# Experts by halves of the batch, with the second attention's beginning between the later phases

## The reference

```python
capacity = max(1, int(Sz * CAP_FACTOR / E) + 1)
scores = jax.nn.softmax(jnp.einsum('bsd,ed->bse', x, router_w), axis=-1)
gate_vals, sel_idx = jax.lax.top_k(jnp.swapaxes(scores, 1, 2), capacity)
tokens = x[b_idx, sel_idx]
h = jax.nn.gelu(jnp.einsum('becd,edh->bech', tokens, w1) + b1[None, :, None, :], approximate=False)
y = jnp.einsum('bech,ehd->becd', h, w2) + b2[None, :, None, :]
out = jnp.zeros_like(x).at[b_idx, sel_idx].add(y * gate_vals[..., None])
```

## Time and profile before

| | |
|---|---|
| median of three runs | 796.57 us |
| span of the profiled execution | 801.9 us (its only time; no other is given for it) |
| PE busy | 644.6 us, 80% of the span |
| DVE busy | 548.5 us, 68% |
| POOL busy | 361.2 us, 45% |
| ACT busy | 353.9 us, 44% |
| mean granted clock of PE | 0.925 of full speed |

### The profile page before, as it was taken

One profiled execution on the slowest core, in us unless ns is written; L12 is line 12 of the kernel. 1 busy time (PEld: TensorE's weight loads), 2 busy tenths in 40 slices (PEclk: granted clock), 3 DMA queues, 4 the chain that ended last, 5 costly groups with the idle time before them and its releaser, 6 DMA issues.

```text
span 801.9 us, 14622 instructions
## 1 busy us (share of the span) xinstructions
PE 644.6 (80%) x4312; PEld 398.9 (50%) x4345; DVE 548.5 (68%) x1808; ACT 353.9 (44%) x764; POOL 361.2 (45%) x513
## 2 busy tenths in 40 slices
PE   1489898997206699999795569899999999999795
PEld 1246666664103478877584223454545454544453
DVE  8378888888691133243336797889898989898454
ACT  0323232320711222233231205776777777767883
POOL 0176555552007587788862102434434344333342
PEclk9999999999657799999997667999999999999998
DMA  9300000000231222223324440203131221300011
GB/s 297 106 1 1 0 1 0 0 1 1 78 106 49 32 43 41 41 42 43 44 25 102 52 59 4 60 16 50 26 41 31 34 41 25 50 15 2 17 54 40
DMA packets 42937, 33.51 MB, mean 42 GB/s; under 512 B 4144, under 2 KB 39520, under 8 KB 42864
## 3 DMA queue, kind: packets, MB, share of 16 engines
q1 hardware_dynamic: 32528, 24.62, 14.3%
q0 software_dynamic: 8992, 7.38, 6.4%
q10 hardware_dynamic: 1344, 0.62, 0.3%
HBM read 13.87 MB, written 8.91 MB: 28 GB/s over the span
## 4 chain that ended last, share of the span: by engine, by line
PE 45%; DVE 20%; POOL 13%; issue 12%; ACT 3%; DMA 2%; SPq 1%; DVEq 0%; ACTq 0%; POOLq 0%
PE bank L1982 8%; DVE masked L1574 7%; POOL x_dram L950 7%; POOL x_row L943 6%; PE wide L1969 5%; PE wide L639 4%; PE bank L1914 3%; PE bank L611 3%; PE wide L640 3%; PE bank L1121 2%; DVE st L292 2%; DVE mx L1574 2%; DVE prod L389 2%; PE wide L621 1%; PE bank L1994 1%
## 5 line engine op out<-in xcount | busy, mean ns | idle before, releaser
L1761 ACT ACTIVATE pexp<-wide 128x512 f32<-128x512 f32 (+2 forms) x384 | 181.3, 535 | 73.4 <-PE wide L1969 70.2
L1685 POOL TENSOR_SCALAR_AFFINE_SELECT pexp<-pexp 128x256 f32<-128x256 f32 x256 | 106.1, 418 | 185.7 <-ACT pexp L1761 183.7
L1574 DVE CUSTOM_DVE_ANT_0 masked<-bank,mask_qk 128x384 f32<-128x384 f32 (+3 forms) x356 | 154.0, 481 | 18.6 <-PE bank L1914 17.7
L1969 PE MATMUL wide<-qT,kTe 128*128 128x256 bf16 (+3 forms) x501 | 119.7, 301 | 6.6 <-ACT pexp L1761 2.5
L1092 ACT ACTIVATE hT<-wide,b1T 128x512 f32<-128x512 f32 x64 | 43.8, 687 | 147.1 <-PE wide L1112 112.8
L1914 PE MATMUL bank<-kTm,qT 128*128 128x384 bf16 (+3 forms) x348 | 87.1, 318 | 18.9 <-DVE mx L1574 9.4
L950 POOL DMA_INDIRECT x_dram<-yg,row_u x48 | 76.2, 1588 | 31.5 <-DVE yg L999 18.6
L1574 DVE CUSTOM_DVE_ANT_0 masked<-wide,mask_qk 128x256 f32<-128x256 f32 (+3 forms) x156 | 74.2, 498 | 17.8 <-PE wide L1914 17.8
L943 POOL DMA_INDIRECT x_row<-xln_dram,row_u x64 | 62.4, 975 | 52.8 <-DVE slot_tok L819 33.6
L1982 PE MATMUL bank<-pexp,vx 128*32 128x512 f32 (+3 forms) x1024 | 83.9, 439 | 0.5 <-POOL pexp L1685 0.5
L1121 PE MATMUL bank<-w_sb,hT 128*128 128x128 f32 x512 | 71.6, 283 | 5.0 <-issue 5.0
(11 more groups left out here) (273 smaller groups left out, 1056.0 us busy)
## 6 DMA issues: line engine op xcount, KB each, us to landing
qT<-qp SPq DMA_DIRECT2D x144, 64.0 KB
x_sb<-in_L_attn_x SPq DMA_DIRECT2D x8, 256.0 KB, 6.7
w_sb<-in_L_ffn_w SPq DMA_DIRECT2D x1, 2048.0 KB, 13.3
xln_dram<-rx SPq DMA_DIRECT2D x8, 256.0 KB, 2.3
out_x<-x_sb SPq DMA_DIRECT2D x7, 256.0 KB, 2.3
x_dram<-x_sb SPq DMA_DIRECT2D x6, 256.0 KB, 3.6
x_sb<-x_dram SPq DMA_DIRECT2D x6, 256.0 KB, 2.8
x_row<-xln_dram,row_u POOLq DMA_INDIRECT x64
```

The source lines that it names most:

```text
L1574: ins = nc.vector.tensor_tensor_reduce(out=masked[:, n % 4, at], in0=bank_of(n)[:, at], in1=mask_qk[:, T - w:T], scale=1.0, scalar=LEAST, ...
L1685: nc.gpsimd.affine_select(out=pexp[:, at, :, 0:P], in_=pexp[:, at, :, 0:P], pattern=[[0, 2], [1, P]], compare_op=ALU.is_ge, fill=0.0, base ...
L1761: nc.scalar.activation(pexp[:, exp_slot(b, 2 * step + h // 2), h % 2:h % 2 + nh, 0:w], scores_bank(b, m)[:, 0:nh * w].rearrange("p (h t) - ...
L1969: ins = nc.tensor.matmul(scores_bank(b, m)[:, hh * w:(hh + 1) * w], kTe[:, par, j * P:(j + 1) * P], qT[:, b % QB, 4 * qd + h + hh, j * P:T ...
```

## The change

The experts' phases go through all eight experts with sequences 0 to 3 (phases 0 to 7, the first half), then with sequences 4 to 7. PE scatters sequences 0 and 1 in the first half and 4 in the second, one after another into the same PSUM bank of the sequence over all experts, with one addition to x at the end; DMA scatters 2 and 3, then 5 to 7. `SEQ` becomes 0 to 7. The stages of the last slots and the rests lie in phases 1 to 7 (one rest in phase 10); the rests of 5 to 7 are added to x before it is copied to DRAM. Transposed rows get one PSUM bank and are copied by ACT, hidden groups have two banks, not three.

The beginning of the second attention moves between the phases of the second half: sequence 0's square root and normalizing behind phase 8, its transposes, queries and keys in phase 9, sequence 1's one phase later, the maxima of sequence 0 from the third slot of phase 10 to phase 14, the shift and the first 11 units of sequence 1 in phase 15. In it DVE splits the keys, which POOL did. ACT loads its gelu table again after each of the two square roots. The statistics of sequences 4 to 7 stand in turn 0, and their square root with two table loads on ACT; sequences 5 to 7 are loaded back after the shift rows. Buffers of the attention that are now used among the experts become lasting ones, and the buffer of the routing's normalized x shares memory with the hidden values.

The core of the diff:

```diff
-        BY_PE = (6, 7)
-        SEQ = BY_PE + BY_DMA
+        FIRST, SECOND = tuple(range(G)), tuple(range(G, B))
+        PE_FIRST, PE_SECOND = FIRST[:2], SECOND[0]
+        DMA_FIRST, DMA_SECOND = FIRST[2:], SECOND[1:]
+        SEQ = FIRST + SECOND
...
-        psX, psH, psYe = (bank[0], bank[1]), (wide[:, 0:512], wide[:, 512:1024], bank[5]), (bank[2], bank[7])
-        side = bank[6]
+        psX, psH, psYe = bank[5], (wide[:, 0:512], wide[:, 512:1024]), (bank[2], bank[7])
+        side = bank[0]
+        sums = dict(zip(BY_PE, (bank[1], bank[6], bank[6])))
+        half_of = lambda p: FIRST if p < E else SECOND
...
+        LAST_AT = {1: LAST_XT, 2: LAST_HIDDEN, 4: LAST_OUTPUT, 5: LAST_T}
+        REST_AT = dict(zip(((6, 0), (6, 2), (6, 3), (7, 0), (7, 2)), BY_DMA))
+        REST_SUM_AT = dict(zip(((7, 1), (7, 3), (10, 3)), BY_PE))
...
             for k in range(NT):
-                ins = nc.tensor.matmul(into[:, k * D:(k + 1) * D], place[:, BY_PE.index(b), k * P:(k + 1) * P],
-                                       yg[:, e % 2, b, :], start=True, stop=True)
+                ins = nc.tensor.matmul(sums[b][:, k * D:(k + 1) * D], place[:, place_of(e, b), k * P:(k + 1) * P],
+                                       yg[:, e % 2, b, :], start=(e, k) == (0, 0),
+                                       stop=(e, k) == (E - 1, NT - 1))
...
+            for p in range(E + 2, PHASES):
+                dve_moe_place(dve, p - E, PE_SECOND)
+                for i in range(G):
+                    dve_start_max(dve, p, i, "X")
+                    if i == G - 1:
+                        dve_moe_gated(dve, p)
+                    dve_start_max(dve, p, i, "Y")
...
+            for n in range(2):
+                if (p, i) == STD_AT[n]:
+                    act_std(act, *((0, 1, 3), (1, G, 4))[n])
+                    act.wait_ge(s_shift.sem, s_shift.total(3 + n))
+                    act_xln(act, n)
+                    act_preset(act, ACT.Gelu)
...
                     if i == 0 and p + 2 < PHASES:
-                        pe_moe_xT(pe, e + 1, half)
-                    pe_moe_side(pe, e, half, i)
+                        pe_moe_xT(pe, p + 2)
+                    pe_start_max(pe, p, i, "X")
+                    pe_moe_side(pe, p, i)
                     pe_moe_output(pe, p, i)
-            for b in BY_PE:
-                pe_moe_scatter(pe, E - 1, b)
+                    pe_start_max(pe, p, i, "Y")
+            pe_scores(pe, 0, 0)
+            pe_moe_scatter(pe, E - 1, PE_SECOND)
...
+        SECOND_STATS_AT = {3: 4, 7: 5, 8: 6, 9: 7}
+        SECOND_STD_STEP, SECOND_SHIFT_STEP = 10, 12
...
             sp_shift_rows(sp, 0)
+            for b in DMA_SECOND:
+                x_from_dram(sp, b)
```

More of the change, by code:

```diff
@@ L63, in build @@
     QB = 3
+    TOP = P // 8
+    HALF = T // 2
     with ExitStack() as ctx:
@@ new lines, in build, with x_to_dram, x_from_dram @@
+        REST_SUM_AT = dict(zip(((7, 1), (7, 3), (10, 3)), BY_PE))
+        fill_no = {key: n + 1 for n, key in enumerate([("last", n) for n in LAST_AT.values()]
+                                                      + [("rest", b) for b in BY_DMA])}
+        def x_to_dram(sp, b, half):
+            sp.dma_start(of_sequence(x_dram, b), x_sb[:, b]).then_inc(m_xw[half], 16)
+        def x_from_dram(sp, b):
+            sp.wait_ge(m_sc[b], 16 * E)
+            sp.dma_start(x_sb[:, b], of_sequence(x_dram, b)).then_inc(m_back[b], 16)
@@ new lines, in moe_act, with pe_moe_xT @@
+        def moe_act(act):
+            act_moe_xT(act, 0)
+            for c in range(HC):
+                act_moe_hidden(act, 0, c)
+            act_moe_xT(act, 1)
+            for p in range(PHASES - 1):
+                for i in range(G):
+                    act_moe_hidden(act, p + 1, i)
+                    if i == 0 and p + 2 < PHASES:
+                        act_moe_xT(act, p + 2)
+                    act_moe_aside(act, p, i)
+        def pe_moe_xT(pe, p):
+            pe.wait_ge(m_g[p % 4], 16 * G * (p // 4 + 1))
+            if p:
+                pe.wait_ge(m_xg, p)
@@ L1579, in build, with dve_start_max, pe_start_max @@
         bank_in_turn = lambda n: bank[unit_bank[n]]
-        bank_at_start = lambda n: psM4[n % len(psM4)]
+        start_max, at_unit = {}, 0
+        for p in range(E + 2, PHASES):
+            if p == PHASES - 1:
+                assert at_unit == NM
+                at_unit = 0
+            for i in range(G):
+                three = p >= E + 4 and i < G - 1 and (p, i) != (PHASES - 2, G - 2)
+                for spot in "XY":
+                    n = 0 if (p, i) < (E + 2, 2) else 2 if three and spot == "X" else 1
+                    start_max[p, i, spot] = range(at_unit, at_unit + n)
+                    at_unit += n
+        assert at_unit == AHEAD
+        TWO_BANKS = start_max[E + 4, 0, "X"].start
+        start_bank = (lambda n: bank[1] if n < TWO_BANKS else bank[n % 2], lambda n: bank[1 + n % 2])
+        def dve_start_max(dve, p, i, spot):
+            b = int(p == PHASES - 1)
+            dve_max(dve, b, start_max[p, i, spot], start_bank[b])
+        def pe_start_max(pe, p, i, spot):
+            b = int(p == PHASES - 1)
+            for n in start_max.get((p, i, spot), ()):
+                if b == 0 and n == 0:
+                    pe.wait_ge(m_added, 1)
+                elif b == 0 and n == TWO_BANKS:
+                    pe.wait_ge(q_kTm.sem, q_kTm.at(1, 1))
+                elif b == 0:
+                    pe.wait_ge(q_mx.sem, q_mx.at(0, n - 1 if n > TWO_BANKS + 1 else min(n, TWO_BANKS)))
+                elif n == 0:
+                    pe.wait_ge(q_mx.sem, q_mx.at(0, NM))
+                elif n == 1:
+                    pe.wait_ge(m_y, PHASES - 1)
+                else:
+                    pe.wait_ge(q_mx.sem, q_mx.at(1, n - 1))
+                pe_max_unit(pe, b, n, start_bank[b](n))
         def dve_shift(dve, b):
@@ L1921, in pe_max @@
                 i, before = unit_bank[n], unit_before[n]
-                if before >= 0:
+                if b == 1 and before < AHEAD:
+                    pe.wait_ge(q_mx.sem, q_mx.at(1, AHEAD))
+                    if bank[i] is sums[PE_SECOND]:
+                        pe.wait_ge(m_added, len(BY_PE))
+                elif before >= 0:
                     pe.wait_ge(q_mx.sem, q_mx.at(b, before + 1))
```

483 lines of the change are left out of this document (242 added, 241 removed).

## The result

The changed kernel took 778.62 us (777.54 to 780.5), the kernel before 796.58 in the same comparison: a ratio of 0.9773, 95% interval 0.9758 to 0.9788, so 18.0 us faster. 772 was forecast, and the range of 758 to 787 holds the result. In the profiled execution of the change the time is 778.48 us at a span of 776.7.

A forecast was written before the change was run, and what follows sets the result against it. Experts bound by POOL without asides, PE with them; a 62.2 us attention beginning is nearly a chain, DVE in front. 29.0 us saved, less 1.7 for clock and 2.5 for turn 0, gives 24.8 less: 772 us, range 758 to 787.

The forecast's parts named there:

- gating 0: Start of the first half: the first gating begins at 269.9 us, nothing ahead of it changing but the row-gathering order.
- phase 1: First half: 11.2 us in the earlier trace becomes 13.0 us with two scatters.
- phases 2 to 7: First half: 55.5 us of phases, 13.7 of last-slot stages and 7.7 of seven rests.
- phase 10: Second half: 17.0 us, about 5 of it PE waiting for key parts, the first keys' copy and the second queries.
- phase 15 to the first scores: End of the second half: 12.5 us, with gating 14, last unit, shift, maxima and gating 15 on DVE.
- 1.7 back for the clock: After PE's waits: one loss of 1.7 us from slower running, bounded by none and four such losses.
- turn 0: DVE gets 6 us more against 7.8 idle; 2.5 us charged, bounds 0 and 9; growth above 8 means wrong reasons.
- four rivals: Waits vanish, 756 us, 0.12; waits double, 787, 0.10; PE's clock stays low, 814, 0.04; nothing moves, 0.02.
- have the 14 us from the first queries to the first unit: Second half: SP's nine row transfers per half of the queries, 0.7 us each, have that time.
- certain: Phases 9 and 10: ACT's table loads, 1.28 us each, named against the rival in which waits vanish.
- covered by PE's 99: Second half: POOL's 16 gathers and 24 scatters, 66 us, plus two small copies, lie under PE's 99 us.
- a clock above 0.9: Sign in the changed profile: PE's granted clock above 0.9 from 280 us on.

The follow-up runs named there:

- the second profile: The kernel before, profiled again with no edit; span 796.8 us, first gating at 263.14.
- e5: Changed kernel with two buffers for the query parts, SP instead of ACT waiting for the earlier row transfers; 776.95 us, ratio 0.9729.
- e7: Changed kernel with plain copies for both square roots of phases 8 and 9, their four table loads gone (roots left out); 777.29 us, ratio 0.9754.
- e8: Changed kernel with turn 0's statistics of sequences 4 to 7 taken of one tile in four (work left out); 776.02 us, ratio 0.9725.
- e6: Changed kernel with a plain copy for turn 0's square root, both table loads gone (root left out); 776.13 us, ratio 0.9743.
- e2: Changed kernel with POOL's last three scatters moved behind the first causal masks of turn 0's steps 1, 2 and 3; 776.88 us, ratio 0.9763.
- e10: Changed kernel with two query-part buffers and plain copies for the square roots of phases 8 and 9 (roots left out); 774.09 us, ratio 0.9727.
- e4: Changed kernel as it is, run and profiled again as the level for other runs; 779.78 us, ratio 0.9774.

## Why the prediction was right, and where it was not

The measured steps are those of the changed kernel's first profile (gating 7 at 352.15, 8 at 361.39, 9 at 373.35, 10 at 393.82, 11 at 406.33, 14 at 440.59):

| step | forecast us | measured us |
|---|---|---|
| gating 0 | 269.9 | 263.75 |
| phase 1 | 13.0 | 9.6 |
| phases 2 to 7 | 76.9 | 78.8 |
| phase 8 | 9.25 | 9.24 |
| phase 9 | 12.6 | 11.96 |
| phase 10 | 17.0 | 20.5 |
| phase 11 | 12.8 | 12.5 |
| phases 12 to 14 | 34.7 | 34.3 |
| phase 15 to the first scores | 12.5 | 11.9 |
| gating 0 to the first scores, against before | -27.3 (-29.0, and 1.7 back for the clock) | -29.05, the clock's loss in it |
| turn 0 | +2.5 (0 to 9) | +8.1, +9.5 from the scores |

- **The shape was right.** The first half grew (88.4 us from gating 0 to 7, against 76.5 before, 72.5 in the second profile), with PE busy without a gap and all asides in this half; the second half took in the attention's beginning, with PE idle for 12.9 us of it where the sum had 15 us of waits; PE, not POOL, is in the chain; the granted clock is 0.97 in the second half. None of the four rivals happened.
- **Gating 0** was put where a disturbed execution had it. That shifts the forecast times of day of the changed kernel and not the gain; the choice to subtract the gain from the median of the runs was right, since the profile's own difference of 25.2 us has a stall of one execution in it.
- **Phase 1** was priced from the same disturbed row (11.2 us in the earlier trace rows, plus two scatters). With the 7.85 us of the second profile the same working gives 7.85 + 1.78 = 9.6, which is what came. It was 3.4 us too much.
- **Phases 2 to 7** were priced 1.9 us too low together. Phase 3, with nothing aside, took 9.24 us, as priced; those with a stage took 16.38 instead of 16.09, and rests 1.2 to 1.3 each instead of 1.1.
- **Phase 10** was 3.5 us too low, by three things. PE's three waits are 1.62 + 1.95 + 1.90 = 5.5 us, against 5 charged. The rest that goes into the third sum lies in this phase, and the step counted only the seven of the first half: 1.1 us. And some 1.6 us are half clock, for which the prediction had 1.7 as a term of its own. One reason failed: the step said that SP's row transfers "have the 14 us from the first queries to the first unit". They do, for the unit; but the second sequence's queries need the same buffer, and they come first. e5 and e7 show this wait, and e7 shows that the table loads, called "certain", cost phase 10 nothing while it stood.
- **Phase 15** had gating 15 ahead of the first scores; it came behind them, in turn 0, so 11.9 us instead of 12.5 is no gain.
- **Phase 1 and phase 10 cancel** (3.4 too much, 3.5 too little), so the gain up to the first scores, 29.05 us against 27.3, came out close partly by luck.
- **Turn 0 is the step that failed,** and its error is as large as that of the time (6.8 us). 2.5 us were charged, with growth by more than 8 named as the mark beyond which the reasons are wrong; it grew by 8.1 from copy to copy and 9.5 from the scores. So by the prediction's own mark its reasons are wrong here, though the time lies in the range. The prediction compared DVE's 6 us of new work with DVE's 7.8 us of idle time in the old turn 0. Three quarters of the statistics alone are worth 1.6 us (e8), more beside the other two edits; and two costs were not on DVE. The table loads were counted as ACT's busy time and set against nothing, though PE waits for the exponential behind them: 2.6 us, the half clock among them (e6). And POOL's last three scatters stand in POOL's queue ahead of turn 0's first masks: 1.9 us (e2). The prediction had POOL "covered by PE's 99" us, which holds for the half as a whole and not at its end. From the forecast 24.8 us less: 1.75 more were won up to the first scores, 7.0 fewer in turn 0 (9.5 instead of 2.5) and 0.6 fewer in the later turns, which gives 18.9 by the profiles; 18.0 were measured, and the last 0.9 was not traced.
- **The clock.** In the changed kernel's first profile PE's clock fell once in phase 10, behind the third of three waits, and once in turn 0. By stage, its phases 9, 10 and 11, and 12 to the scores:

```profile
361.39:373.35 11.96, 11.02 (x67) 8.07 (x66) 7.85 (x28) 9.48 (x18) 9.39 (x8) 1.00 0.33 59
373.35:393.82 20.47, 14.99 (x87) 11.22 (x86) 7.51 (x31) 8.78 (x18) 9.20 (x9) 0.92 0.58 93
393.82:406.33 12.51, 12.19 (x67) 8.08 (x67) 8.06 (x26) 3.94 (x6) 9.12 (x8) 0.86 0.72 89
406.33:452.46 46.13, 40.02 (x261) 29.06 (x259) 35.80 (x141) 11.30 (x17) 18.98 (x13) 1.00 0.24 25
```

For the fall in phase 10 the sum had the right size: from the keys and values to the end of the phase PE took 3.64 us (390.18 to 393.82), against 2.09 in e5 and in e10 at full rate there, so it cost 1.55 us, and 1.7 were charged. PE stayed at half clock into phase 11 (0.86), where the prediction had named a clock above 0.9 as a sign, but this cost the phase nothing. In e5 the phase is as long at a clock of 1.00, since PE then waits 0.53 us for DVE's maxima and 1.19 for its key parts, the wait that the sum had there:

```profile
392.85:405.35 12.50, 10.72 (x66) 7.38 (x66) 8.05 (x26) 3.83 (x6) 9.11 (x8) 1.00 0.73 89
```

The fall in turn 0, behind the wait of 1.95 us for the exponential, was not in the sum. The second profile of the same kernel (e4) has a fall behind the second wait of phase 10 as well as behind the third; these are the outputs behind each, which take 1.06 us at full rate:

```profile
382.36 1.71 PE L1221 MATMUL bank<-w_sb,hT 128*128 128x128 f32 x8
...
393.61 2.05 PE L1221 MATMUL bank<-w_sb,hT 128*128 128x128 f32 x8
```

The Trainium skill (TensorE: Matmul & The Clock Gate, section on HAM oscillation) describes a PE that waits for a DMA at every tile and starts each one cold. The prediction took this over to all its waits, but those of the section are longer than the three of phase 10 (1.62, 1.95 and 1.90 us); of these, one was followed by a fall in the first profile and two in the second, so neither "every wait" nor the sum's "one" holds for each execution.

## What to carry to other kernels

When work moves beside other work, list for each moved step the buffers that it writes and who still reads them: a transfer that is early enough for its own reader can be late for the next writer of its source. At the seam between two stages, look at each engine's queue by itself: what a queue has left over from the first stage delays the second one's first small instruction, however idle the engine is on average. If an engine feeds the bound just in time, price its table loads by how long the bound waits behind them, not by that engine's idle share. And profile the kernel twice before a price is taken from a row next to a stall.

## What the hardware showed that was not expected

- Waits of nearly the same length were followed by a fall of PE's clock in one execution and not in another. In phase 10 it fell behind the third of three waits (1.62, 1.95, 1.90 us) in the changed kernel's first profile, behind the second and the third (1.94, 1.78) in its second, and behind the second (1.94) in e5; the wait of 1.84 us in turn 0 was followed by a granted clock of 0.62 in e7 (456.40 to 459.00, 2.65 us for the values) and of 1.00 in the change (1.71). Which it will be could not be told from the rows here.
- Eighteen transfers, issued 0.65 us apart, let the next query copy start 18.4 us behind the first in e2 (369.41 to 387.84) and 20.5 us in e4, with the same instructions up to there: 2.1 us, nearly the 2.2 by which phase 10 differs between the two (19.54 and 21.74).
- One profiled execution of the kernel before stood some 7 us longer ahead of its first gating than another of the same code, and yet needed the same 212 us from there to the shift.
